# Graph network on one core: a one-hot operand and a weighting operand read from PSUM, and one PSUM bank each for attention transposes and queries

## The reference

```python
edge_index = jnp.stack([src, dst])
x = _layernorm(x + _L0_gnn_ref(x, edge_index, edge_attr_2, ...))       # 4-head attention over two projections
x = _layernorm(x + _L1_gnn_ref(x, W_self, W_neigh, src, dst))          # top-32 of a projection, mean over dst
x = _layernorm(x + _L2_gnn_ref(x, Wf, Wb, ..., src, dst, edge_type_16, 0, 0))  # 16 relations, sums over dst and over src
x = _layernorm(x + _L3_gnn_ref(x, edge_index, ...))                    # two attention layers, 8 heads of 16

# one attention layer of L3
q, k, v = (rowE @ qT), (colE @ kT), (colE @ vT)       # rows = edge_index[0], cols = edge_index[1]
att = jnp.clip(jnp.einsum('ehd,ehd->eh', q, k), -10.0, 10.0)
expAtt = jnp.exp(att)
attNorm = jax.ops.segment_sum(expAtt, rows, num_segments=n)[rows]
res = ((expAtt / (attNorm + 1e-08))[..., None] * v).reshape(-1, d)
agg = jax.ops.segment_sum(res, rows, num_segments=n)
```

## Time and profile before

| what | value |
|---|---|
| median of 3 runs | 9883.51 us (9871.92 to 9894.19) |
| profiled execution: its span, from first to last instruction | 7939.2 us |
| its own time beside the span | not listed apart; the runs' median is 1944.3 us more than the span |
| POOL busy | 5744.1 us (72%) |
| PE, PEld busy | 4723.0 us (59%), 3281.5 us (41%) |
| DVE busy | 4571.4 us (58%) |
| ACT busy | 1304.4 us (16%) |
| mean granted clock of the tensor engine | 0.790 of full speed |

### The profile page before, as it was taken

The page is one execution under the profiler, slowest core; times in us unless marked ns, Lnnn a source line. Parts: engine busy times, 40 slices in busy tenths (PEclk is TensorE's granted clock), DMA queues, the critical chain, the costliest instruction groups (busy, mean ns, idle before and its releaser), DMA issues.

```text
span 7939.2 us, 105932 instructions
## 1 busy us (share of the span) xinstructions
PE 4723.0 (59%) x17448; PEld 3281.5 (41%) x17449; DVE 4571.4 (58%) x11380; ACT 1304.4 (16%) x5226; POOL 5744.1 (72%) x5938
## 2 busy tenths in 40 slices
PE   4555653355555890077777556655666665666664
PEld 3333431233333440044444334433555554555553
DVE  6788887355444440055555544444666666666666
ACT  4666650000000000000000000001211111111111
POOL 4777777777777777777777777774677774777773
PEclk7777676677777995599999776676888887888887
DMA  3332330233333351055555333332333333333332
GB/s 100 56 57 55 57 50 21 66 97 98 101 103 87 117 161 31 23 149 157 158 157 158 100 102 103 102 103 67 101 102 101 101 102 80 100 101 100 101 101 64
DMA packets 513845, 751.71 MB, mean 95 GB/s; under 512 B 232770, under 2 KB 365943, under 8 KB 513271
## 3 DMA queue, kind: packets, MB, share of 16 engines
q0 software_dynamic: 252096, 604.80, 28.1%
q1 hardware_dynamic: 261686, 146.25, 6.1%
HBM read 624.19 MB, written 126.41 MB: 95 GB/s over the span
## 4 chain that ended last, share of the span: by engine, by line
POOL 51%; issue 35%; DMA 5%; ACT 3%; DVE 2%; PE 2%; POOLq 1%; ACTq 0%; DVEq 0%; SPq 0%
POOL rows L233 41%; POOL slots_s_dram L513 10%; DMA rows<-table,gidx 3%; ACT msg L577 2%; PE ps L273 1%; ACT big L565 1%; PE ps L359 1%; DMA rows<-table2f,gidx 0%; DVE big L671 0%; DMA rows<-table3b,gidx 0%; DMA rows<-table3a,gidx 0%; POOLq L77 0%; DMA rows<-table2b,gidx 0%; DVE x_sb L680 0%; DVE acc L261 0%
## 5 line engine op out<-in xcount | busy, mean ns | idle before, releaser
L261 DVE TENSOR_TENSOR acc<-acc,ps 128x257 f32 (+3 forms) x4992 | 1879.7, 377 | 1980.8 <-PE ps L273 1788.6
L273 PE MATMUL ps<-rows,onehot 128*128 128x257 f32 (+1 forms) x4992 | 1689.7, 498 | 1664.6 <-DMA rows<-table2f,gidx 602.2
L273 PEld LDWEIGHTS ps<-rows,onehot 128*128 128x128 f32 x4992 | 1162.6, 244 | 2277.8 <-issue 1711.8
L233 POOL DMA_INDIRECT rows<-table,gidx x1664 | 1647.6, 990 | 512.7 <-issue 458.7
L273 PE MATMUL ps<-msg,onehot 128*128 128x136 f32 (+1 forms) x4992 | 1282.9, 418 | 536.9 <-ACT msg L577 345.6
L273 PEld LDWEIGHTS ps<-msg,onehot 128*128 128x128 f32 x4992 | 981.6, 253 | 835.1 <-issue 378.6
L233 POOL DMA_INDIRECT rows<-table3a,gidx x832 | 820.9, 987 | 362.4 <-issue 251.3
L233 POOL DMA_INDIRECT rows<-table3b,gidx x832 | 829.3, 997 | 333.2 <-issue 251.3
L233 POOL DMA_INDIRECT rows<-table2b,gidx x832 | 821.2, 987 | 269.1 <-issue 251.6
L513 POOL DMA_INDIRECT slots_s_dram<-stage,stage_row x806 | 798.7, 991 | 274.4 <-issue 226.9
L233 POOL DMA_INDIRECT rows<-table2f,gidx x832 | 788.6, 948 | 253.4 <-issue 253.4
(11 more groups left out here) (211 smaller groups left out, 4229.8 us busy)
## 6 DMA issues: line engine op xcount, KB each, us to landing
table2f<-big SPq DMA_DIRECT2D x80, 640.0 KB, 4.8
table2b<-msg SPq DMA_DIRECT2D x200, 256.0 KB, 2.3
rows<-table,gidx POOLq DMA_INDIRECT x1664
slots_d<-recs_d SPq DMA_DIRECT2D x832, 2.5 KB
rows<-table2f,gidx POOLq DMA_INDIRECT x832
rows<-table2b,gidx POOLq DMA_INDIRECT x832
rows<-table3a,gidx POOLq DMA_INDIRECT x832
rows<-table3b,gidx POOLq DMA_INDIRECT x832
```

The lines of the kernel that those rows point to most:

```text
L233: nc.gpsimd.indirect_dma_start(out=rows[:, j, 0:width], out_offset=None, in_=table[:, :], in_offset=bass.IndirectOffsetOnAxis(ap=gidx[:, h ...
L261: nc.vector.tensor_tensor(acc[:, bass.ds(b * width, width)], acc[:, bass.ds(b * width, width)], ps[:, bank + k, 0:width], ALU.add).then_in ...
L273: nc.tensor.matmul(ps[:, bank + k, 0:width], onehot[:, h, k, :], rhs, start=True, stop=True).then_inc(sem(of(s, "tile_sum")), 1)
```

## The change

Three things change.

1. `iota` is copied to a corner of PSUM before a stage, and `one_hot` reads it there: bank 4 for `e1` and `e2b`, bank 1 for `e3a` and `e3b`. `e2f` keeps reading SBUF, as `e0` does, whose comparison is written out apart. Four copies of 128x128 are added.
2. In the attentions ACT computes the exponents twice, once to PSUM (bank 3, `p_ps`) and once to `res3` as before. The weighting reads the copy in PSUM. It waits for `att_p_ps` of one group more than it needs, so that ACT does not write the bank while DVE reads it, and ACT takes its exponents ahead of its row numbers.
3. That needs banks 1 and 3. So all transposes go through bank 0 and all queries through bank 2. `transposes(n)` waits for the copy-out of n-1, no longer n-2, and `queries(n)` for the product of n-1, no longer n-2.

```diff
+        here_sum, here_att = ps[:, 4, 0:P], ps[:, 1, 0:P]
+        here = {"e1": here_sum, "e2f": iota[:, :], "e2b": here_sum, "e3a": here_att, "e3b": here_att}
+        p_ps = ps[:, 3, 0:R * G * H3].rearrange("p (r w) -> p r w", r=R)
...
-            nc.vector.tensor_tensor(onehot[:, h, :, :], bc(iota[:, :].unsqueeze(1), [P, G, P]),
+            nc.vector.tensor_tensor(onehot[:, h, :, :], bc(here[s].unsqueeze(1), [P, G, P]),
...
-                nc.scalar.activation(oneT[:, h, :, :], ps[:, h % 2, :].rearrange("p (g e) -> p g e", g=G), ACT.Copy)\
+                nc.scalar.activation(oneT[:, h, :, :], ps[:, 0, :].rearrange("p (g e) -> p g e", g=G), ACT.Copy)\
...
+                nc.scalar.activation(p_ps[:, h, :], att[:, 1 + h % 2, :], ACT.Exp).then_inc(sem("att_p_ps"), 1)
...
             def step(n, h, left):
+                exponents(n, h)
                 if left > 3:
                     index(n + 3, (h + 3) % R)
-                exponents(n, h)
...
-                after(pe, "att_oneT", start + n - 1)
+                after(pe, "att_oneT", start + n)
...
-                after(pe, "att_qk", start + n - 1)
+                after(pe, "att_qk", start + n)
...
             transposes(0, 0)
+            queries(0, 0)
             transposes(1, 1)
-            queries(0, 0)
...
                 after(dve, "att_p", start + n - 1)
+                after(dve, "att_p_ps", start + n - 1)
...
-            def weighted(n, h):
+            def weighted(n, h, left=NG):
+                after(dve, "att_p_ps", start + n + (2 if left > 1 else 1))
                 after(dve, "att_p", start + n + 1)
...
-                    bc(res3[:, h, :, D:W3].unsqueeze(3), [P, G, H3, HD]), ALU.mult).then_inc(sem("att_res"), 1)
+                    bc(p_ps[:, h, :].rearrange("p (g a) -> p g a", a=H3).unsqueeze(3), [P, G, H3, HD]), ALU.mult).then_inc(sem("att_res"), 1)
...
+                link(nc.vector.tensor_copy(here_sum, iota[:, :]))
                 dve.wait_ge(sem("d1_stored"), TABLE_STORED)
...
+                link(nc.vector.tensor_copy(here_sum, iota[:, :]))
                 dve.sem_inc(sem("e2f_done"), 1)
...
+                    link(nc.vector.tensor_copy(here_att, iota[:, :]))
                     link(nc.vector.memset(acc[:, 0:NB * W3], 0.0))
```

More of the change, by code:

```diff
@@ L732, in transposes @@
                 after(pe, "tile_onehot", groups0[s] + n + 1)
-                after(pe, "att_oneT", start + n - 1)
+                after(pe, "att_oneT", start + n)
                 for k in range(G):
-                    last = nc.tensor.transpose(ps[:, h % 2, k * P:(k + 1) * P], onehot[:, h, k, :], ident[:, :])
+                    last = nc.tensor.transpose(ps[:, 0, k * P:(k + 1) * P], onehot[:, h, k, :], ident[:, :])
                 last.then_inc(sem("att_tr"), 1)
@@ L743, in queries @@
                     b = of_tile[k]
-                    last = nc.tensor.matmul(ps[:, 2 + h % 2, k * D:(k + 1) * D], oneT[:, h, k, :],
+                    last = nc.tensor.matmul(ps[:, 2, k * D:(k + 1) * D], oneT[:, h, k, :],
                                             q_sb[:, bass.ds(b * D, D)], start=True, stop=True)
@@ L775, in step @@
                 after(dve, f"rows_ready{h}", gathered(s, n, h))
-                nc.vector.tensor_tensor(qk3[:, h, :, :], ps[:, 2 + h % 2, :].rearrange("p (g d) -> p g d", d=D),
+                nc.vector.tensor_tensor(qk3[:, h, :, :], ps[:, 2, :].rearrange("p (g d) -> p g d", d=D),
                                         rows4[:, h, :, 0:D], ALU.mult).then_inc(sem("att_qk"), 1)
@@ L803, in att_dve @@
             att_groups(dve, step)
-            weighted(NG - 1, (NG - 1) % R)
+            weighted(NG - 1, (NG - 1) % R, 1)
             add_tiles(dve, s, block_s, NG - 2, 4, W3)
```

## The result

The changed kernel takes 10034.1 us (10030.1 to 10040.5, 4 runs), the kernel before, in the same batch, 9877.9 us. The ratio is 1.0154, with a 95% interval of 1.0140 to 1.0168: 156 us slower, where 124 us less were forecast.

The account below looks back on a forecast made before the run. The prediction took POOL's gathers (indirect DMAs) to bound the kernel. Sum stages -48.6, attentions -76.0 and ends +0.5 made -124 us, from 9883.5 to 9760 us, with an 8-in-10 range of 9725 to 9797.

Parts of the forecast that it names:

- The step that failed: Whole kernel: the 1944.3 us between profiled span (7939.2 us) and runs' median (9883.5) stay unchanged by the edits.
- That POOL bounds the kernel: Gather loops: POOL's indirect DMAs run without a hole, 832 gathers taking 1037 us a stage; PE and DVE aren't the bound.
- one operand in PSUM is enough: DVE operations beside gathers: with either operand in PSUM, a gather starting under them keeps its 0.95 us.
- The new forms: One-hot and weighting reading PSUM: 0.69 us expected for both; at half speed, 0.7 us more for each.
- The second exponents at nothing: ACT in the attentions: 0.23 us each, 208 a stage, hidden in the loop; only 0.5 us exposed at the ends.
- The single banks at nothing: Attention transposes and queries, one bank each: over 2 us to spare in a step, cost 0.
- The attentions' -76.0: One-hot and weighting from PSUM in e3a and e3b: all excess gather time goes, 33.8 + 42.2 = 76.0 us.
- Rival A: Ranking and ends shift: e1's stalls change 17 us either way, e2f's one-hots may lose 24; 9801 or 9743 us; chance 0.13.
- The wait and ACT's order, "Cost 0": Attentions: weighting waits for the current step's exponents, made ahead of row numbers; 0.81 us is available, so cost 0.
- Rival D: Attentions: slow reads of spread PSUM operands make DVE the bound; 10276 us at a third of the speed; chance 0.03.
- Rival B: Time outside the span belongs to the same loops and stalls grow with it: -154 us, 9730 us; chance 0.11.
- the sum-stage term of 48.6 us: One-hot from PSUM in e1 and e2b: gathers lose their stalls under it, 48.6 us less.

Follow-up runs that it names:

- e0_before: The kernel before, unchanged, profiled once more at the slower pace: 9887.8 us, ratio 1.0002.
- e2_onehot: Kernel before plus single banks for transposes and queries and the attentions' one-hot from PSUM, at the faster pace: ratio 0.9912.
- e1_sum: Kernel before with the one-hot from PSUM in stages e1 and e2b alone, at the slower pace: ratio 1.0012.
- e2_weight: Kernel before plus all the attention's edits except the one-hot from PSUM, sum stages as before, at the faster pace: ratio 0.9998.
- e2_order: Kernel before plus single banks and ACT's exponents ahead of its row numbers, at the faster pace: ratio 0.9999.
- e2_wait: Kernel before plus single banks, ACT's exponents first, and the SBUF weighting waiting for the next group's exponents, at the faster pace: ratio 0.9999.
- batch 3: Slower-pace runs beside the kernel before (9886.6 us): the changed kernel again, ratio 1.0166, and three kernels with parts of its edits.
- f1_after: The changed kernel again, against the kernel before at the slower pace: ratio 1.0080.
- f1_weight: Kernel before plus all the attention's edits except the one-hot from PSUM, sum stages as before, at the slower pace: ratio 1.0065.
- batch 4: Slower-pace runs beside the kernel before (9829.0 us): the changed kernel again, ratio 1.0080, and three variants with some edits left out.
- e3_onehot: Kernel before plus single banks and the attentions' one-hot from PSUM, at the slower pace: ratio 0.9976.
- f1_best: Changed kernel with one exponents instruction, to SBUF, where the weighting reads it; against the kernel before at the slower pace: ratio 1.0016.
- f1_expo: Kernel before plus the attention's edits, but one-hot and weighting read SBUF (exponents still made twice), at the slower pace: ratio 0.9942.
- e3_banks: Kernel before with single banks for the attentions' transposes and queries alone, at the slower pace: ratio 0.9978.
- e3_wait: Kernel before plus single banks, ACT's exponents first, and the SBUF weighting waiting for the next group's exponents, at the slower pace: ratio 0.9927.

## Why the prediction was wrong

**The step that failed** is "The runs' median, 9883.5, lies 1944.3 us above it, time that the page doesn't show and that I take as unchanged". `e0_before` shows 1.8 us outside its span (9915.0 less 9913.2). The difference was another pace: a stage of 832 gathers that takes 1075 us in the earlier trace rows takes 1427 us in `e0_before`, an execution at the pace of those that were timed. What its engines wait for are late products of the tensor engine, which no term of the sum has, and instead of 124 us less the kernel takes 156 more. A gap of 20% between a profiled span and the median should have stopped the argument, since every term of the sum was bound to that trace's bottleneck.

**That POOL bounds the kernel** holds in the trace that was read, and was borne out at that pace by `e2_onehot` (70 us of 76). At the slower pace POOL stands idle 606 us of `e3a`, of which only some 254 are its own gaps (1075 less 821 in the earlier trace rows), and 24 us saved on its gathers come back as 26 us of idling (`e1_sum`).

**Right:** one operand in PSUM is enough (longest gather 0.963 us, a gather of 0.95 under the new weighting). The new forms take 0.69 and 0.68 us. Against the inference of the Trainium skill ("SBUF — State Buffer", section "Who interferes with whom"), a one-hot with both operands in SBUF does hold up gathers (1.12 us beside 0.95), and moving one operand ends it. The second exponents at nothing: right at the faster pace (`e2_weight`, 0.9998), and nothing against it at the slower. The single banks at nothing: right at the faster pace, where `e2_order` and `e2_wait` hold them at 0.9999, and 0.2 to 0.3% too dear at the slower.

**The attentions' -76.0:** 70 us at the faster pace, and all of it from the one-hot; the weighting gives 1 us, within the interval. At the slower pace the same edits cost. Rival A's one-hots on the gathers of `e2f` came, in POOL's busy time there: 787.7 us in the trace that was read, 795.6 in `e0_before`, 803.3 in the changed kernel.

**The wait and ACT's order, "Cost 0":** 0.9999 at the faster pace. At the slower they gain 0.5%.

**Not foreseen by any rival:** at the slower pace the weighting's operand in PSUM costs 1.1% (109 us) while the operation itself gets no longer. Rival D had slower by slow reads from PSUM; the reads are not slow. Rival B had the right doubt, that the missing time belongs to the loops, but scaled the gain with it, where it should have asked whether POOL was still the bound.

**The sum at the slower pace**, as differences of the ratios to the kernel before: single banks -0.2%, order and wait -0.5% (batch 3), second exponents 0 (across batches), weighting from PSUM +1.2%, all one-hots from PSUM +0.15% on top (`f1_after` 1.0080 beside `f1_weight` 1.0065, batch 4). That makes 0.65%, near the 0.80% of batch 4, and leaves the other half of the 1.54% and 1.66% that the changed kernel lost in the first comparison and in batch 3 without an account. Nor do the parts simply add: the attentions' one-hots from PSUM cost nothing over single banks alone (`e3_onehot`), and all one-hots cost 0.7% over order and wait (`f1_best` beside `f1_expo`).

**Open.** Why an operand in PSUM makes the loop longer at the slower pace is not settled. Every edit there that frees the gathers left the time alone or lengthened it, which speaks for a loop that falls into another rhythm against the late products. The shift of the waits from transposes and queries to the sums fits, and so does the one-hot that holds up hardly a gather in `f1_weight`. But that the rhythm costs the time is argued, not shown. A direct hindrance of the tensor engine by DVE's reads from PSUM was not excluded, as no run read from PSUM without also freeing gathers; against it stands `e3_onehot`, whose one-hot reads PSUM in each step and costs nothing over `e3_banks`. What makes the products late on some chips was not found. The changed kernel as a whole was not run at the faster pace, so the sum-stage term of 48.6 us is untested where it should count.

`e2_onehot` / `e3_onehot`, single banks and the attention's one-hot from PSUM, is ahead of the kernel before at either pace (0.9912 and 0.9976), and of the changed kernel at the slower. At the slower pace alone `e3_wait` is the best, 0.9927.

## What to carry to other kernels

Before any sum is made on a trace, set its span beside the timed median; when they are 20% apart, the trace shows another regime, and the question is which engine is the bound in the timed one. Of an operation that disturbs another engine, look at where in its period the other one's starts fall: at the faster pace the one-hot alone sat on a gather's start, and the weighting's move gave nothing there and cost 1.1% at the slower. An edit that frees an engine should be measured where that engine isn't the bound too: here such edits gained nothing at the slower one, and several went with a longer loop.

## What the runs showed of the hardware

- The same kernel took 7937 us on one chip and 9823 to 9887 us on three others, with granted clocks of 0.79 and 0.70 to 0.71. The one-hot takes 692 ns at both.
- A gather that starts under a DVE operation of 0.69 us with both operands in SBUF, and not in its last 0.13 us or so (an estimate from the earlier trace rows), takes longer than 0.95 us (1.10 to 1.26 us in the rows shown); with one operand in PSUM none of the attentions' 1664 is over 0.963 us.
- At the slower pace the tensor engine's products came up to 8.6 us after matmuls whose records end within 1.2 us, at the 2.4 GHz level, and 6.5 us after they began at the 1.2 GHz level.
- With six of a group's twelve products left out and the sums narrowed, the granted clock in `e3a` went from 0.70 (`e0_before`) to 0.50, PE's busy time there from 799 to 622 us, and the kernel gained only 1.7%.
